# Two mixture-of-experts layers: from all experts on all rows to blocks of 128 rows sorted by expert

## The reference

```python
x = x + _L0_gnn_ref(_layernorm(x), edge_index, ...)   # attention over 17408 edges
x = x + _L0_ffn_ref(_layernorm(x)[None], ...)[0]      # layer 0 of the experts
x = x + _L1_gnn_ref(_layernorm(x), ..., src, dst)
x = x + _L1_ffn_ref(_layernorm(x)[None], ...)[0]      # attention, then layer 1

# _L0_ffn_ref: 8 experts, D = 512, H = 256
raw_weights = jax.nn.softmax(flat_x @ gate_w + gate_b, axis=-1)
top_w, top_idx = jax.lax.top_k(raw_weights, 2)
gate_output = (one_hot(top_idx, 8) * top_w[..., None]).sum(axis=-2)
h = jax.nn.gelu(jnp.einsum('td,edh->teh', flat_x, w1) + b1, approximate=False)
expert_out = jnp.einsum('teh,ehd->ted', h, w2) + b2
combined = jnp.einsum('ted,te->td', expert_out, gate_output)

# _L1_ffn_ref, after attention: t is the layer-normed x
idx = jnp.argmax(t @ Wg + bg, axis=-1)
h = jax.nn.gelu(jnp.einsum('td,edh->teh', t, W1) + b1, approximate=False)
y = jnp.einsum('teh,ehd->ted', h, W2) + b2
moe = jnp.einsum('ted,te->td', y, one_hot(idx, 8))
return _layernorm(x + moe, g2, beta2)
```

## Time and profile before

| | us |
|---|---|
| median of 3 runs | 1368.66 |
| lowest, highest | 1366.26, 1372.76 |
| the profiled execution, whole | 1371.85 |
| its span, first to last instruction | 1370.1 |
| TensorE, VectorE, ScalarE, GpSimd busy | 1063.7, 672.9, 378.4, 626.8 |

### The profile page before, as it was taken

One profiled execution on the slowest core, in us unless ns is written; L12 is line 12 of the kernel. 1 busy time (PEld: TensorE's weight loads), 2 busy tenths in 40 slices (PEclk: granted clock), 3 DMA queues, 4 the chain that ended last, 5 costly groups with the idle time before them and its releaser, 6 DMA issues.

```text
span 1370.1 us, 14365 instructions
## 1 busy us (share of the span) xinstructions
PE 1063.7 (78%) x4784; PEld 834.6 (61%) x4784; DVE 672.9 (49%) x1231; ACT 378.4 (28%) x544; POOL 626.8 (46%) x422
## 2 busy tenths in 40 slices
PE   3276799104878999978888789999998845999994
PEld 2155678003645888856677567777776623588883
DVE  4544430004643243373522657777777776242448
ACT  0201012003422212121222046655656522212120
POOL 1587888882302343200722227777766632233430
PEclk9987799656977999998999879999999986799997
DMA  9524222228700111002311220010000041111101
GB/s 265 107 17 26 16 1 1 0 0 219 210 2 31 31 54 47 15 31 77 108 39 31 84 62 16 17 31 17 23 16 17 1 138 31 31 46 46 46 0 61
DMA packets 79841, 68.86 MB, mean 50 GB/s; under 512 B 32288, under 2 KB 63264, under 8 KB 78512
## 3 DMA queue, kind: packets, MB, share of 16 engines
q1 hardware_dynamic: 59056, 63.96, 16.2%
q0 software_dynamic: 20736, 4.27, 5.8%
HBM read 47.17 MB, written 16.85 MB: 47 GB/s over the span
## 4 chain that ended last, share of the span: by engine, by line
PE 54%; DVE 16%; POOL 13%; DMA 8%; issue 6%; ACT 3%; SPq 0%; DVEq 0%; ACTq 0%; POOLq 0%
PE PS L241 41%; POOL edge_table L452 12%; DMA edge_table<-count,index 5%; DVE neg_max L1128 3%; PE PS L1461 2%; PE PS L1476 2%; PE PS L1450 2%; DVE APL L798 2%; PE PS L1366 2%; PE PS L1475 2%; DMA edge_table<-zeros 1%; DVE stats L806 1%; DVE XN L831 1%; DVE XN L1196 1%; DMA CT<-edge_table 1%
## 5 line engine op out<-in xcount | busy, mean ns | idle before, releaser
L464 POOL CAST WH<-RAW 128x512 fp32r<-128x512 f32 x94 | 66.4, 707 | 482.3 <-PE PS L241 376.8
L452 POOL DMA_INDIRECT edge_table<-count,index x136 | 214.5, 1577 | 87.4 <-issue 37.1
L538 POOL TENSOR_SCALAR AP__136<-AP__136,rden 128x1024 f32<-128x1024 f32 x64 | 181.9, 2848 | 84.8 <-DVE rden L1133 84.1
L241 PE MATMUL PS<-XTH,WH 128*128 128x512 f32 x480 | 169.3, 419 | 9.0 <-DVE XTL L798 6.7
L241 PE MATMUL PS<-XTL,WH 128*128 128x512 f32 x480 | 164.1, 408 | 0.0
L241 PE MATMUL PS<-XTH,WL 128*128 128x512 f32 x480 | 162.0, 403 | 0.0
L466 POOL TENSOR_TENSOR WL<-RAW,WH 128x512 fp32r<-128x512 f32 x94 | 138.2, 1470 | 11.8
L798 DVE TENSOR_TENSOR HL<-HF,HH 128x1024 fp32r<-128x1024 f32 x32 | 46.9, 1469 | 174.5 <-ACT HH L574 174.5
L241 PEld LDWEIGHTS PS<-XTH,WH 128*128 128x128 f32 x480 | 95.0, 201 | 32.9 <-issue 12.6
L666 ACT ACTIVATE HF<-PS,b 128x1024 f32<-128x1024 f32 x32 | 35.8, 1118 | 273.8 <-PE PS L241 273.8
L241 PEld LDWEIGHTS PS<-XTL,WH 128*128 128x128 f32 x480 | 96.3, 201 | 20.8
(11 more groups left out here) (190 smaller groups left out, 1951.4 us busy)
## 6 DMA issues: line engine op xcount, KB each, us to landing
edge_table<-zeros SPq DMA_DIRECT2D x2, 4096.0 KB, 22.8
RAW<-in_L_ffn_w SPq DMA_DIRECT2D x32, 256.0 KB, 2.7
RAW<-in_L_ffn_W SPq DMA_DIRECT2D x32, 256.0 KB, 2.7
CT<-edge_table SPq DMA_DIRECT2D x8, 512.0 KB, 5.9
CT<-edge_table POOLq DMA_DIRECT2D x8, 512.0 KB, 6.9
counts<-CT SPq DMA_DIRECT2D x8, 512.0 KB, 6.8
CG<-counts SPq DMA_DIRECT2D x8, 512.0 KB, 3.4
RAW<-in_L_gnn_W SPq DMA_DIRECT2D x16, 256.0 KB, 2.7
```

Of the source, the lines that this page charges most:

```text
L241: got = pe.matmul(o, lhs, r, start=first and j == 0, stop=last and j == 2)
L452: gp.indirect_dma_start(out=tables[r], out_offset=bass.IndirectOffsetOnAxis(ap=index[:, c:c + 1], axis=0), in_=count[:, c:c + 1], in_offse ...
L464: gp.tensor_copy(wh, RAW[:, raw, :]).then_inc(w_hi, 1)
L538: gp.tensor_scalar(AP_[:, i % 4, :], AP_[:, i % 4, :], rden[:, i % 4:i % 4 + 1], None, ALU.mult).then_inc(B["norm"], 1)
```

## The change

Both expert layers work on rows sorted by expert. The pairs (row, chosen expert), 2048 in layer 0 and 1024 in layer 1, are laid into blocks of 128 of one expert each. With 8 experts at most 23 and 15 blocks are needed whatever the gates are, and so many are always computed.

*Routing.* From the gates VectorE and TensorE compute the rank of each row within its expert (products with a triangle and with ones), the first block of each expert, the place of each pair, and by one more product (`lane_of`, `column_of`) the inverse: for each place the row. Results are `expert_i` (a block's expert), `gather_i` (row to fetch) and `scatter_i` (where the result goes; places without a row go to spare rows). TensorE reads its block's expert from memory into a register, all 23 or 15 before the loop; VectorE one per block within the loop.

*Weights.* All of W1 and W2 of a layer lie in SBUF, in high part and rest, before the loop starts. SyncE loads them in sixteen 512 KB pieces, ScalarE makes the high parts (128x1024 each, `w1_hi`, `w2_hi`), GpSimd the rests (`expert_lo`). The biases b1 lie as rows (B1).

*Rows.* SyncE saves XN to DRAM (`xn_d`). For each block GpSimd gathers 128 rows of 2 KB into one of three buffers BX; TensorE turns them (4 transposes), ScalarE and VectorE form BTH and BTL; TensorE computes 128x256 hidden units, row-major (12 matmuls of 256 columns); VectorE adds the bias row, ScalarE applies GELU; 2 transposes, BHH and BHL; 6 matmuls of 512 columns; ScalarE copies the result to BY (two buffers), and GpSimd scatters it to `y_d` in DRAM. When all blocks have landed, SyncE loads the results in row order (YT), two per row in layer 0, one in layer 1, and VectorE adds them (layer 0: times the gate) and takes the statistics.

Beside this: the loops of `Fori` in the first attention and of TensorE and ScalarE in the second graph layer are written out, some semaphores are merged, GpSimd fills constant tables for the routing after the edge scatters, g2 is loaded apart, and the addition of beta2 moves to VectorE, tile by tile inside layer 1's loop.

The diff, cut to its core (in this order: constants, SyncE in layer 0, GpSimd, ScalarE's `moe` with the weights and the loop, TensorE's `moe`, the removed addition):

```diff
+    CHOICES = (2, 1)
+    BLOCKS = tuple((k * N + NEXP * (P - 1)) // P for k in CHOICES)
...
+        wait(A["m1"], NT)
+        load_w1(a["L0_ffn_w1"])
+        wait(A["av_ps"], NT)
+        load_w2(0, a["L0_ffn_w2"], 0, 6)
+        wait(LN["xn"], 2 * NT)
+        save_rows(0)
+        load_w2(0, a["L0_ffn_w2"], 6, NEXP)
+        results(0)
...
+        def expert_lo(which):
+            for e in range(NEXP):
+                wait(M["w_hi"], 2 * NEXP * which + e + 1)
+                gp.tensor_tensor(W1L[:, e, :, :], W1R[:, e, :, :], f(W1H[:, e, :, :]), ALU.subtract).then_inc(M["w_lo"], 1)
+            for e in range(NEXP):
+                wait(M["w_hi"], 2 * NEXP * which + NEXP + e + 1)
+                gp.tensor_tensor(W2L[:, e, :, :], W2R[:, e, :, :], f(W2H[:, e, :, :]), ALU.subtract).then_inc(M["w_lo"], 1)
+        def expert_rows(which):
+            first, n = which * BLOCKS[0], BLOCKS[which]
+            def gather(b):
+                g = first + b
+                if g >= 3:
+                    wait(M["x_ps"], g - 2)
+                gp.indirect_dma_start(
+                    out=BX[:, g % 3, :], out_offset=None, in_=xn_d[:, :],
+                    in_offset=bass.IndirectOffsetOnAxis(ap=gather_i[:, b:b + 1], axis=0)).then_inc(M["rows_in"][g % 3], 16)
+            wait(M["routed"], routed(which, "scatter"))
+            wait(M["xn_saved"], 16 * which + 16)
+            for b in range(3):
+                gather(b)
+            for b in range(n):
+                if b + 3 < n:
+                    gather(b + 3)
+                g = first + b
+                wait(M["y_sb"], g + 1)
+                gp.indirect_dma_start(
+                    out=y_d[:, :], out_offset=bass.IndirectOffsetOnAxis(ap=scatter_i[:, b:b + 1], axis=0),
+                    in_=BY[:, g % 2, :], in_offset=None).then_inc(M["rows_out"][g % 2], 16)
+        expert_lo(0)
+        expert_rows(0)
...
+            for e in range(4):
+                w1_hi(e)
+            transposed(turn, LTH)
+            for e in range(4, NEXP):
+                w1_hi(e)
...
+            rows_hi(0)
+            rows_hi(1)
+            gelu(0)
+            for b in range(n):
+                hidden_hi(b)
+                if b + 2 < n:
+                    rows_hi(b + 2)
+                if b:
+                    out_rows(b - 1)
+                if b + 1 < n:
+                    gelu(b + 1)
+            out_rows(n - 1)
...
+            for t in range(4, NT):
+                bias_rows(t)
+            pe.wait_ge(M["routed"], routed(which, "experts"))
+            experts = [pe.value_load(expert_i[0:1, b:b + 1], min_val=0, max_val=NEXP - 1) for b in range(nb)]
+            pe.wait_ge(M["acc"], which * NT + NT)
...
+            rows_transposed(0)
+            rows_transposed(1)
+            hidden(0)
+            for b in range(nb):
+                hidden_transposed(b)
+                if b + 2 < nb:
+                    rows_transposed(b + 2)
+                if b + 1 < nb:
+                    hidden(b + 1)
+                out_rows(b)
...
-        gp.tensor_tensor(X[:, :, :], X[:, :, :], rows1[:, 3, :].unsqueeze(1).to_broadcast([P, NT, D]),
-                         ALU.add).then_inc(F["beta"], 1)
```

More of the change, by code:

```diff
@@ new lines, in load_w2, with save_rows @@
+        def load_w2(which, w2, first, last):
+            for half, w2_share in enumerate((96, 32)):
+                wait(M["w_in"][half], which * (64 + w2_share) + 64)
+            for e in range(first, last):
+                sp.dma_start(W2R[:, e, :, :], w2[e].rearrange("(k p) n -> p k n", p=P)).then_inc(M["w_in"][e // 6], 16)
+        def save_rows(which):
+            sp.dma_start(xn_d.rearrange("(t p) d -> p t d", p=P), XN[:, :, :]).then_inc(M["xn_saved"], 16)
+            wait(M["lg_ps"], 2 * which + 2)
@@ new lines, in results @@
+        def results(which):
+            total = sum(BLOCKS[:which + 1])
+            for r in range(2):
+                wait(M["rows_out"][r], 16 * ((total + 1 - r) // 2))
+            for g in range(4):
+                for c in range(CHOICES[which]):
+                    sp.dma_start(YT[:, c, 2 * g:2 * g + 2, :],
+                                 y_d[c * N + 2 * g * P:c * N + (2 * g + 2) * P, :].rearrange("(t p) d -> p t d", p=P)).then_inc(M["y_in"][g], 16)
+        expert_biases("L0_ffn_b1")
@@ new lines, in moe, with rows_hi @@
+            copy(gatesT[0:NEXP, :], PS[0:NEXP, 4:6, :].rearrange("p a b -> p (a b)"), M["gt"])
+            for e in range(3, NEXP):
+                w2_hi(e)
+            first, n = which * BLOCKS[0], BLOCKS[which]
+            def rows_hi(b):
+                g = first + b
+                if g >= 2:
+                    act.wait_ge(M["h_ps"], g - 1)
+                act.wait_ge(M["x_ps"], g + 1)
+                copy(BTH[:, g % 2, :, :], PS[:, g % 2, :].rearrange("p (k n) -> p k n", k=KT), M["x_hi"])
@@ L1303, in _ @@
         p_transposes(0, 0)
-        with pe.Fori(0, NT // 2 - 1) as i:
+        for i in range(NT // 2 - 1):
             p_transposes(i, 1)
@@ L1311, in _, with moe @@
         values(NT // 2 - 1, 1)
-        def moe(turn, which, ready, before, u0):
+        def moe(turn, which, ready, before):
             transposes(turn, XN, ready, before)
@@ L1361, in moe, with bias_rows @@
             got.then_inc(M["gt_ps"], 1)
[L1362 to L1363 removed]
+            def bias_rows(t):
                 if t >= 4:
@@ new lines, in hidden @@
+            def hidden(b):
+                g = first + b
+                if b == 0:
+                    pe.wait_ge(M["w_lo"], 2 * NEXP * which + NEXP)
+                pe.wait_ge(M["x_lo"], g + 1)
+                e = ds(experts[b])
+                for k in range(KT):
+                    w_hi_ = W1H[:, e, k, :].rearrange("p a n -> p (a n)")
+                    w_lo_ = W1L[:, e, k, :].rearrange("p a n -> p (a n)")
+                    got = three_pass(pe, [PS[:, 2 + g % 2, 0:HID]], BTH[:, g % 2, k, :], BTL[:, g % 2, k, :], [w_hi_], [w_lo_],
+                                     k == 0, k == KT - 1)
+                got.then_inc(M["h_ps"], 1)
```

618 lines of the change are left out of this document (377 added, 241 removed).

## The result

The changed kernel takes 1379.34 us (median of 6 runs, 1374.83 to 1382.64), the kernel before 1368.88 us beside it (6 runs): ratio 1.0076, 95% interval 1.0052 to 1.0100. It is slower, by 10.5 us; the interval lies wholly above 1. Forecast were 1422 us, that is 53 us more, with a range of 1350 to 1500.

The account below looks back on a forecast made before the run. TensorE's matmuls bound the expert loops before; the gather-scatter ring would bound them after. Layer 0 +70.1 and layer 1 -17.2 gave +52.9 on 1371.85, so 1424.8; the median stands 3.2 lower, so 1422 us, range 1350 to 1500.

Parts of the forecast that it names:

- the ring: Block loops: BY to next BY through scatter, gather, transposes and ScalarE's copies takes 4.0 or 4.4 us plus gather landing.
- loop starts: Ahead of both loops: subtractions, routing, bias rows and register loads put the starts at about 477 and 1205.5 us.
- to the first scatter: Start of each loop: filling the ring up to BY of block 0 costs 12 to 18 us, taken as 15.
- T: Time per block in both expert loops, set by the ring: 7.9 us, bounds 5.2 and 11.2.
- GpSimd's issue: In the ring: issuing one scatter takes 1.85 us, from the spacing of indirect DMA instructions; lower bound 1.15.
- the landing of the gather: In the ring: a gather takes 3.7 us from issue to landing; bounds 1.9 and 6.9.
- Rival B: Block loops: gathers land like an ordinary 256 KB load, 2.7 us, T = 6.9, 30 us less, 1392; chance 0.21.
- Layer 1's opening: Ahead of layer 1's loop: gather 0 at about 1188, then bias rows 8.5 and loads 9.0, loop at about 1205.5.
- a third of the round trip: TensorE's register loads ahead of the loops: 0.6 us each, 13.8 and 9.0 us in all.
- Rival C: Ahead of the loops: ring as forecast, but register loads and subtractions cost little, 45 us less, 1377; chance 0.11.
- Rival D: Block loops: 2 KB rows are dear to issue or land, T = 11, +93 us, 1515; chance 0.16.
- Rival A: Block loops: quick row transfers, T = 5.2 or less, 81 us off, 1341, faster than before below T = 6.1; chance 0.22.

Follow-up runs that it names:

- e1: The changed kernel with ScalarE copying BY of block b-1 ahead of BTH of block b+2: 1324.16 us, ratio 0.9696 to the kernel before.
- e4: The changed kernel with TensorE's register loads of the experts' numbers done twice: 1400.40 us, ratio 1.0257 to the kernel before.
- e10: e9 with ScalarE copying the gate weights ahead of the transposed rows: 1260.76 us, ratio 0.9196 to the kernel before.
- e5: The changed kernel with GpSimd's weight subtractions cut to 2 columns, TensorE reading the high part instead of the rest: 1339.44 us, ratio 0.9789 to the kernel before.
- e6: The changed kernel with each layer's eight W2 subtractions moved behind the first three gathers: 1360.45 us, ratio 0.9940 to the kernel before.
- e7: e2 with TensorE loading the experts' numbers one per block in its loop, two ahead of use: 1266.57 us, ratio 0.9254 to the kernel before.
- e14: e12 with gather buffers counted within a layer: 1250.56 us, ratio 0.9148 to the kernel before.
- e13: e10 with gather buffers counted within a layer: 1253.90 us, ratio 0.9156 to the kernel before.
- e9: e2, e6 and e7 together on the changed kernel: 1268.22 us, ratio 0.9259 to the kernel before.
- e12: e10 with four of layer 1's W2 subtractions ahead of the first gathers and four behind: 1258.97 us, ratio 0.9200 to the kernel before.
- e2: The changed kernel with four gather buffers instead of three, each gather issued one block earlier: 1276.49 us, ratio 0.9348 to the kernel before.

## Why the prediction was wrong

The mechanism was right where it mattered most: the ring of ScalarE's order, GpSimd's order and three buffers, TensorE idle for part of each block, granted clock below 1.00 (though at 0.92 not well under it), layer 0 losing more than layer 1 wins, and a win over the kernel before once the period falls (e1). The amount was wrong by a factor of five: 53 us more were forecast, 10.5 measured. A small difference of two large sums (+70.1 and -17.2) stood on some fifteen terms, and most were taken too dear. Term by term, in us:

| term of the sum | layer 0: forecast, found | layer 1: forecast, found |
|---|---|---|
| loop starts (from 0; from the first gate instruction) | 477, 476.5 | 47.0, 36.1 |
| to the first scatter | 15, 14.7 | 15, 12.8 |
| ring periods, 19 and 11 | 150.1, 132.5 | 86.9, 79.0 |
| last three blocks | 11, 8.3 | 11, 8.3 |
| last scatter lands | 3.8, 3.2 | 3.8, 2.8 |
| results come back | 4.7, 5.0 | 3.5, 3.7 |
| VectorE's tiles | 18.8, 19.1 | 12.6, 12.3 |
| end | 680.4, 659.3 | 179.8, 154.9 |

**The step that failed first is T.** The sum put 7.9 us for a block, the bounds were 5.2 and 11.2; it is 6.97 and 7.18. That is 17.6 + 7.9 = 25.5 of the 49.9 us: the mechanism was right, the size of this term was not. Of its parts the copies and transposes were right (forecast 1.23 + 0.2 and 0.72 to 1.12; in the chain above 1.36 from BTH to the scatter, 0.75 for the transposes). Too dear were GpSimd's issue, 1.85 taken from the spacing of the edge scatters, where a row transfer takes 1.29 (539.19 to 540.48), and the landing of the gather, 3.7 against 3.3 to 3.6 in the chain (3.4 from issue to landing in the median of 38, 3.2 to 4.4). The edge scatters add to what they find and the row transfers only copy, so they were not the same operation; the bound that I had noted, 1.15 for the issue, was nearer than the value that I took. By the fit of the Trainium skill (DMA: Bandwidth & Descriptors, Anatomy of one DMA) 256 KB would take an estimated 2.6 us: the scatters landed in 2.8, which is near to it, the gathers in 3.4, so for them the measurement decides against it. Rival B, which took the ordinary load's landing and T = 6.9, came to the right period by luck: its landing of 2.7 was 0.7 too short, its issue of 1.85 some 0.6 too long.

**Layer 1's opening**, 10.9 us of the miss. I let the bias rows and the loads follow the first gather. They don't wait for it: they wait for the routing, which ended at 1227.3, and ran beside the last subtractions; the gather went out at 1232.4, at the time forecast, and had landed before TensorE was through with its loads. The loads showed 4.5 us instead of 9.0, since half of them ran under the last bias rows (e4). In layer 0 the loads were also too dear (10.0 us open instead of 13.8), but the first gather went out at 457.4 instead of 453, and with it the bias rows, since here both waited for the routing. I had missed some 4 us by which ScalarE's copy of the gate weights stands behind the last W1 copies (e10). The two errors cancel, so 477 was right by luck of the sum.

**The ends.** The last three blocks took 8.3 us twice, the lower bound of the 8 to 14 given. The filling in layer 1 and the landings add 3.9 us. **Between the layers** the sum had no change (the 0.7 for layer 1's norm is within the 47.0), and the traces show -3.8 against the kernel before: 2.5 of it between the end of the attention and the norm's root, which in the kernel before waited 2.6 us for the load of beta1 and in the changed one for nothing. I had not looked there. Before, the wait is this row:

```profile
1121.39 0.17 DVE L814 TENSOR_SCALAR ve<-mv 128x8 f32<-128x8 f32 x1 [2.63 <-DMA rows<-in_L_ffn_beta]
```

**What was right and is now shown:** that GpSimd's subtractions hold VectorE up (XN 11.86 in place of the 13 forecast, 3.74 without them in e5: 2.0 us for each of the four that fall on it), and that the openings, not only the ring, are worth tens of microseconds (e5, e6, e7). The price of one load, 0.6, met the 0.64 of e4, but "a third of the round trip" had no row behind it: that was luck. Rival C asked whether these openings are cheap: no; without the rests alone the kernel is 40 us faster. Rival D is out: no period came near 11. Rival A named 6.1 us a block as the point from which the change wins. e1, at 5.1 with 0.9696, is beyond it, but the 6.1 rests on the forecast's 52.9; with the 10.5 that were measured the point would lie at an estimated 6.7 (7.05, the mean period of both layers, less 10.5/30).

What stays open: the 7.5 us of the medians' difference that the two profiled executions don't show, why single gathers land after up to 5.8 us in the kernels with four buffers, and whether e14 is faster than e13.

## What to carry to other kernels

In a loop over blocks that go from DRAM to DRAM, look for the ring first: which result must leave before the next input may be asked for, and how many blocks that ring spans. Here a block took 7.0 us, 5.1 with two lines swapped in ScalarE's order and 3.6 with one more buffer, where TensorE's own work sets the pace. That was worth five and ten times what the change itself had moved, and busy shares alone would not have named it: they showed only that no engine was busy all the time. When a forecast is the difference of two large sums, take each term at the row of the same kind of operation, and check whether all errors point one way; and when an edit brings a wait of its own, follow it into every later use of the loop (the wait in e9 to e12 was one that my fourth buffer had brought).

## What the runs showed of the hardware

- A row gather of 128 x 2 KB: 0.98 us of GpSimd, the next DMA instruction 1.29 us after it, landing 3.2 / 3.4 / 4.4 us after issue (least, median, most, 38 of them); a row scatter lands in 2.7 / 2.8 / 3.3 (the changed kernel). With twice the traffic (e2, 144 instead of 76 GB/s) TensorE was still busy for 67.3 of 68.0 us. Where the chain passes a gather in the loops with four buffers, it landed after 3.7 to 5.8 us.
- A register load from SBUF costs TensorE 0.64 us when loads stand in a row, and next to nothing among queued matmuls.
- GpSimd's subtractions of 128 x 1024 stretch a VectorE operation on two SBUF tiles from 0.69 to 2.7 us (0.34 to 2.49 for a small one), a tensor_scalar from 0.18 to 1.82, and leave a reduction at 0.34.
- With the pauses of the ring the granted clock stood at 0.92 and 0.91, not far below 1.00, although TensorE was idle for 40% of the time; in the filling of layer 0's loop (476.4 to 491.0), behind an opening at 0.54, it stood at 0.61, nearer to 1.2 GHz than to 2.4.
